# Flamingo gated cross-attention block: TensorE's values moved behind the first transposed scores, ScalarE's copy of their result behind two exponentials, VectorE's last maxima ahead of the residual sum

## The reference, cut to what matters

```
x = x + tanh(g_xattn) * attention(layernorm(x), ctx)    # 16 heads of 8, softmax over 77 context rows
x = x + tanh(g_ffn) * moe(layernorm(x))                 # shared expert + top 3 of 15 routed experts
attention:
  q, k, v = x w_q', ctx w_k', ctx w_v'
  scores  = q k' / sqrt(8)                              # per head, 128 x 77
  out     = softmax(scores) v, heads side by side, times w_o'
```

## Time and profile before

| | |
|---|---|
| median of the runs | 418.11 us (417.9 to 420.04, three runs) |
| profiled execution | 417.4 us, its span 415.6 us |
| TensorE granted clock, mean | 0.984 |
| busy over the span: TensorE, its weight loads, VectorE, ScalarE, GpSimd | 376.5, 334.3, 301.0, 274.0, 253.1 us |

### The profile page before, as it was taken

How to read it: one execution, slowest core, us unless ns; L and a number is a source line. 1 busy time by engine, 2 the same in 40 slices (tenths; PEclk the granted TensorE clock), 3 DMA queues, 4 the chain that set the end, 5 groups by cost and what they waited for, 6 DMA issues and landing times.

```text
span 415.6 us, 12422 instructions
## 1 busy us (share of the span) xinstructions
PE 376.5 (91%) x3840; PEld 334.3 (80%) x3840; DVE 301.0 (72%) x982; ACT 274.0 (66%) x609; POOL 253.1 (61%) x250
## 2 busy tenths in 40 slices
PE   3589999999999999999899988999999999999940
PEld 1267878787878788878899987899999997999940
DVE  6356877888888889786668976778777762687863
ACT  4338889988889897878666654566666666353500
POOL 6860120176767666675988977307777774777771
PEclk9999999999999999999999999999999999999985
DMA  4659573648363649634355447756666642233322
GB/s 146 180 148 244 175 210 111 165 136 235 118 202 122 190 131 306 225 104 153 123 179 157 155 149 232 231 179 187 193 197 203 200 142 69 77 79 102 82 76 69
DMA packets 57159, 66.30 MB, mean 160 GB/s; under 512 B 9092, under 2 KB 47748, under 8 KB 57096
## 3 DMA queue, kind: packets, MB, share of 16 engines
q1 hardware_dynamic: 49656, 51.49, 41.2%
q0 software_dynamic: 6352, 13.02, 10.8%
q10 hardware_dynamic: 1088, 1.00, 0.8%
HBM read 35.82 MB, written 29.29 MB: 157 GB/s over the span
## 4 chain that ended last, share of the span: by engine, by line
PE 58%; POOL 13%; DVE 8%; issue 7%; DMA 6%; ACT 4%; SPq 2%; POOLq 0%; ACTq 0%; DVEq 0%
PE psum L1493 13%; PE psum L1352 8%; POOL k_heads L625 8%; PE psum L1369 6%; PE psum L1473 4%; PE psum L1474 3%; PE psum L1332 3%; PE psum L1475 3%; PE psum L1463 3%; DVE max_cols L911 3%; POOL q_stack L625 2%; PE psum L1299 2%; PE psum L1342 2%; DMA w_raw<-rows_by_expert 2%; PE psum L1309 2%
## 5 line engine op out<-in xcount | busy, mean ns | idle before, releaser
L563 POOL DMA_INDIRECT rows_by_expert<-xn_all,row_of x96 | 96.1, 1001 | 44.6 <-ACT probs L711 22.5
L803 ACT ACTIVATE probs<-psum,b1c 128x256 f32<-128x256 f32 x152 | 63.8, 471 | 27.5 <-PE psum L1475 26.8
L1493 PE MATMUL psum<-w_all,probs 128*128 x608 | 80.1, 275 | 0.0
L1493 PEld LDWEIGHTS psum<-w_all,probs 128*128 128x128 f32 x608 | 74.2, 191 | 0.2
L625 POOL DMA_INDIRECT k_heads<-outs_by_block,back_row x60 | 57.9, 965 | 23.8 <-issue 16.4
L711 ACT ACTIVATE probs<-psum 77x512 f32<-77x512 f32 x128 | 68.9, 590 | 2.8 <-PE psum L1352 1.5
L911 DVE TENSOR_REDUCE max_cols<-psum 128x4 fp32r<-128x312 f32 x128 | 55.1, 472 | 7.0 <-PE psum L1332 6.5
L1352 PE MATMUL psum<-q_stack,k_heads 128*77 128x128 f32 x512 | 54.3, 243 | 0.8 <-ACT q_stack L703 0.5
L1352 PEld LDWEIGHTS psum<-q_stack,k_heads 128*77 128x77 f32 x512 | 43.8, 151 | 13.0 <-issue 5.6
L1053 DVE CAST w_ring<-w 128x512 fp32r x76 | 34.5, 454 | 22.1 <-issue 21.1
L1473 PE MATMUL psum<-q_parts,w_ring 128*128 128x256 f32 x152 | 49.1, 323 | 1.1 <-DVE q_parts L1041 1.1
(11 more groups left out here) (155 smaller groups left out, 769.5 us busy)
## 6 DMA issues: line engine op xcount, KB each, us to landing
w_raw<-rows_by_expert SPq DMA_DIRECT2D x76, 128.0 KB
outs_by_block<-probs SPq DMA_DIRECT2D x76, 128.0 KB
q_stack<-q_split SPq DMA_DIRECT2D x21, 256.0 KB
q_split<-q_parts SPq DMA_DIRECT2D x7, 512.0 KB, 3.1
k_heads<-k_split SPq DMA_DIRECT2D x90, 39.0 KB
rows_by_expert<-zeros SPq DMA_DIRECT2D x27, 128.0 KB, 3.8
k_split<-w_all SPq DMA_DIRECT2D x8, 312.0 KB, 2.2
x_all<-in_x SPq DMA_DIRECT2D x8, 256.0 KB, 4.9
```

The lines of the kernel that those rows point to most:

```text
L563: nc.gpsimd.indirect_dma_start(xd[:, :], bass.IndirectOffsetOnAxis(ap=row_of[:, r, m:m + 1], axis=0), xn2_all[:, r * GB + m // K, :], None ...
L803: nc.scalar.activation(hid[u % 2][:, c, :], psum[:, 2 + c, 0:BLK], ACT.Gelu, bias=b1c[:, bass.ds(e * CR + (CS + c), 1)]).then_inc(gelu_don ...
L1493: ins = nc.tensor.matmul(psum[:, 4 + u % 2 * 2, b * P:(b + 1) * P], hid[u % 2][:, c, b * P:(b + 1) * P], w2_all[:, bass.ds(expert_of[u] * ...
```

## The change

Three moves, and no instruction more or less. On TensorE, `scores_t(t, 0)`, `scores_t(t, 1)` and behind them `scores(t+1, 2)`, `scores(t+1, 3)` stand ahead of the two waits on the routing and of `values(t-1)`. On ScalarE, `oT_leaves(t-1)` stands behind `exps(t, 0)` and `exps(t, 1)`. On VectorE, `maxima(t+1, 2)` and `(t+1, 3)` stand ahead of the block table's step and of `residual(t-2)`.

```diff
 # ScalarE
+                exps(t, 0)
+                exps(t, 1)
                 if t >= 1:
                     oT_leaves(t - 1)
-                exps(t, 0)
-                exps(t, 1)
 # VectorE
+                if t + 1 < B:
+                    maxima(t + 1, 2)
+                    maxima(t + 1, 3)
                 if t in (TABLE_AT, TABLE_AT + 1):
                     table(0, (t - TABLE_AT) * 2)
                 if t >= 2:
                     residual(t - 2)
-                if t + 1 < B:
-                    maxima(t + 1, 2)
-                    maxima(t + 1, 3)
 # TensorE
                 if t >= 2:
                     turn_on(t - 2)
+                scores_t(t, 0)
+                scores_t(t, 1)
+                if t + 1 < B:
+                    scores(t + 1, 2)
+                    scores(t + 1, 3)
                 if o == 1 and g >= 2:
                     pe.wait_ge(route_step, (g - 2) * ROUTE + 1)
                 if o == 3 and g >= 2:
                     pe.wait_ge(route_step, (g - 2) * ROUTE + 7)
                 if t >= 1:
                     values(t - 1)
-                scores_t(t, 0)
-                scores_t(t, 1)
                 if o == 1 and ahead:
                     front_x(g + 2)
...
                 if t >= 2:
                     project(t - 2)
-                if t + 1 < B:
-                    scores(t + 1, 2)
-                    scores(t + 1, 3)
                 scores_t(t, 2)
                 scores_t(t, 3)
```

## The result

The changed kernel takes 440.81 us (median of four runs, 438.54 to 441.93), against 418.0 us for the kernel before on the same chip: a ratio of 1.053, 95% interval 1.050 to 1.056. It is slower, as forecast, but by 22.8 us and not by 9.7, and above the range of 416 to 434.

A forecast was written before the change was run, and what follows sets the result against it. TensorE was taken to set the attention loop's pace. The terms 3.9 + 0.5 + 4.1 + 1.0 + 1.0 - 1.2 + 0.4 gave 9.7 us more, a forecast of 427.5 us, range 416 to 434.

The forecast's parts named there:

- the 5.00 worked out: Attention loop, kind 3 without a weight copy: a round between first transposed-score matmuls takes 5.00 us against 4.44, +0.56.
- the term that was put at 1.0: TensorE's second pair of scores waits for maxima 0 and 1, only in kind 3 of groups 2 to 4: 1.0 us.
- Kind 3, forecast 3.9 + 0.5: Seven rounds lengthened by ScalarE's later side work, 3.9 us; three of them with a weight copy, another 0.5.
- Kind 2, forecast 4.1 + 1.0: Rounds where apply2 waits for VectorE's chain from turn_o: four at 0.80, three at 0.30, 4.1 us; weight copies 1.0.
- 3.35 was worked out: Kind 2, groups 2 to 5: turn_o 3.35 us behind the round's first transposed-score matmul, waiting for the residual sum.
- put at 2.79: Kind 2: TensorE's order alone puts turn_o 2.79 us behind the round's first transposed-score matmul.
- Kinds 0 and 1, forecast at -1.2: Rounds where TensorE comes last, covering ScalarE's 1.02; moved maxima win: a gain of 1.2 us, between 0.0 and 2.7.
- The stretch behind the last S, forecast at +1.0: Loop's end: the last step gets its values behind its first transposed-score matmul, +1.0 us.
- The scores' wait for maxima spreads to all kinds: Rival "worse", TensorE's scores in the attention loop: 0.4 us in 15 more rounds, +6, giving 434 us; chance 12%.

The follow-up runs named there:

- The transposed scores alone: Changed kernel with the second pair of scores back behind project and VectorE's order of before, ScalarE's copy still behind exponentials 0 and 1: 421.68 us.
- half maxima: Each maximum taken over half of its columns, the other half left out: 433.01 us in the changed kernel, 413.27 us in the kernel before.
- the projection: Changed kernel with only the transposed scores ahead on TensorE and VectorE's order of before, plus the output projection moved ahead of the values: 424.29 us.
- `turn_o`, -0.6%: Kernel before with turn_o put between the transposed scores of part 2 and of part 3, nothing else: 415.98 us, ratio 0.994.
- the run with the statistics in kind 0: Kernel before with turn_o between transposed scores 2 and 3, and VectorE's first-layernorm statistics moved from kind 2 to kind 0 (group 0: kind 1): 422.98 us.

## Why the prediction was wrong

*The direction held, and the mechanism is there.* With the values behind S the round is closed by S, values, ScalarE and `max_rows`. In step 23, where the second pair follows S in 0.60 and hardly waits, the round came to 166.42 - 161.27 = 5.15 against the 5.00 worked out:

```profile
161.27 0.77 PE L1352 MATMUL psum<-q_stack,k_heads 128*77 128x128 f32 x8 [0.49 <-ACT q_stack L703]
161.87 0.63 PE L1332 MATMUL psum<-k_heads,q_stack 128*128 128x312 f32 x2
...
166.42 0.28 PE L1352 MATMUL psum<-q_stack,k_heads 128*77 128x128 f32 x1 [0.46 <-ACT q_stack L703]
```

The transposed scores alone cost 3 us, and undoing ScalarE's move made it worse. But this mechanism alone is only those 3 of the 22.8 us: the direction came out right mostly through the term that was put at 1.0.

*The step that failed* is the one on the second pair: "Only kind 3 of groups 2 to 4 has these statistics ahead; a later S absorbs some, so between 0 and 2.0 for three rounds I take 1.0." The net cost of that pair, with the maxima that go with it, is 440.8 - 421.7 = 19 us. I had looked for steps in which VectorE is unusually late. It need not be late: in the kernel before, maximum 1 ends 1.9 us behind the first scores on average (1.4 to 3.1), and the second pair stood 2.6 behind them. Now it is due 0.61 behind S, which is 1.5 behind the first scores on average. What had covered the maxima until then, the values above all, the same move took away. S to values is 1.45 on average and 1.04 in the rounds that do not wait, and 22 of the 30 rounds do. The price is paid in every kind: against the run with the transposed scores alone, the mean rounds of kinds 0 to 3 are longer by 0.43, 0.32, 0.79 and 0.83 us.

*How the 19 us split* is known only roughly. The waits make S to values 12.4 us longer than 1.04, summed over the 30 rounds; half maxima took 6.4 of that away and 7.8 us of the time, though shorter maxima gave 5.2 us in the kernel before as well, at another place. The pair's own length puts 0.33 (0.71 to 1.04) between S and the values in each round; by the price of the projection, 2.6 us for 0.27, that would come to some 3 us, an estimate. What is left may lie in part in the falls of the clock below; no run separates these parts. The values' delay was passed on through ScalarE where TensorE's next S waited for `max_rows`, in 21 places, 14 of them at the end of a round of kind 2 or 3; in the other rounds the wait for the maxima lengthened TensorE's own order, as I read it.

*Term by term.* Kind 3, forecast 3.9 + 0.5 and 1.0 for the pair, took 7.0. Kind 2, forecast 4.1 + 1.0, took 9.7: `turn_o` came 3.75 behind S in step 14 where 3.35 was worked out. I had the residual sum set it; the sum ended at 3.60, and TensorE's own order, put at 2.79, took 3.75, with 0.71 of the difference ahead of the values. With the transposed scores alone these two kinds took 1.2 and 3.4. Kinds 0 and 1, forecast at -1.2, took +4.1: without the second pair (the transposed scores alone) they gain 1.5, with it that is lost. The stretch behind the last S, forecast at +1.0, took 3.2; in the run with the transposed scores alone, where the values stand there too, it took 0.2.

*A rival that I had priced was the case, and larger:* "The scores' wait for maxima spreads to all kinds", with 434 and 12%. I had let it be 0.4 us in 15 more rounds, 6 us; it was 0.56 on average in 22 rounds, 12.4 us.

*The most used engine.* The Trainium skill, Perfetto Trace Analysis, section Identifying the Most-Contended Engine, calls the engine with the highest occupancy the most contended, and has TensorE's headroom judged by its weight loads' busy share (and its share of the peak arithmetic), not by its matmul busy time. By the busy shares of the earlier trace rows that is ScalarE, with 143.22 us against 133.89. The trace agrees in direction: what ScalarE waits for, the values, grew from 5.6 to 24.7 us. But VectorE's busy time, too, stayed as it was while the loop grew by 20 us, so busy shares alone did not tell the size.

## What to carry to other kernels

An operation that is moved ahead in an in-order queue brings its own waits with it, and everything behind it pays them: before moving it, read how far behind its own trigger its operand is ready in ordinary steps, not only in the late ones, and what covered that distance until now. Moves that fit only together (here the second pair's and the sum's) must be priced together: the sum's alone cost 13 us in the kernel before, the pair's alone 22.6 on top of the transposed scores, both together 19. Here a hole in a full engine was better filled with a neighbour that is ready (`turn_o`, -0.6%) than by reordering what the next round hangs on.

## What the runs showed of the hardware

TensorE's granted clock, which was 1.00 in the whole loop before, fell twice in the changed kernel's, each time behind waits for `max_rows` or maxima: around 91 to 94 and 207 to 210 us, by the columns of the view by windows as above.

```profile
88.00:91.00 3.00, 2.04 (x30) 1.54 (x34) 2.97 (x12) 1.72 (x5) 1.61 (x2) 1.00 0.18 41
91.00:94.00 3.00, 3.00 (x35) 2.53 (x27) 0.84 (x3) 2.04 (x5) 2.08 (x2) 0.52 0.46 175
205.00:207.00 2.00, 0.74 (x7) 0.53 (x7) 1.31 (x6) 1.72 (x4) 0.96 (x1) 1.00 0.20 70
207.00:210.00 3.00, 3.00 (x43) 2.40 (x41) 0.00 (x0) 1.42 (x5) 0.96 (x1) 0.53 0.06 22
```

A granted 0.5 is the lower of the two levels, 1.2 GHz. The 32 matmuls of the values then took 1.94 us, where 1.08 is usual:

```profile
206.77 0.98 PE L1352 MATMUL psum<-q_stack,k_heads 128*77 128x128 f32 x8 [1.26 <-ACT q_stack L703]
207.68 1.94 PE L1369 MATMUL psum<-probs,v_pad 128*32 128x128 f32 x32
```

In the run with the statistics in kind 0 the long wait of step 1 brought a fall, too:

```profile
39.00:45.00 6.00, 2.91 (x9) 1.66 (x9) 2.60 (x13) 0.58 (x1) 1.26 (x2) 0.50 0.83 245
```

So a wait of TensorE can cost twice. I had priced the waits alone. The second fall seems to make up much of the end's 3.2 us: in the five runs with the values behind the last S and no fall there, the stretch behind it is 228.8 to 230.3 us long, in the four with a fall 230.3 to 232.0. No run took the falls away by themselves, so what they cost in all is not shown; about three us at half the clock would lose some 1.5 us each, an estimate from the two windows above.
